# Attention and gated FFN in one kernel: VectorE forms the experts' input, GpSimd takes short row operations

## What is computed

```python
xn = (x - mean) / sqrt(var + 1e-5)                     # per row of 128
s  = causal attention of xn, 16 heads of 8, + xn, layer norm, gamma, beta
# key and query masks: rows of xn whose sum is exactly 0
xl = (xn - mean) * rsqrt(var + 1e-5) * ln_scale + ln_bias     # second norm
x_attn = xl @ attn_w.T + attn_b + xn                   # the experts' input, "xa"
h  = gelu(x_attn @ w1[e] + b1[e]); eo = h @ w2[e] + b2[e]      # 8 experts, 256 rows each
g  = silu(gelu(eo @ next_w.T + next_b))
out = x + s * g
```

## Time and profile before

| | before |
|---|---|
| median of 3 runs | 512.3 us (511.3 to 512.44) |
| the profiled execution, its own time | 512.2 us |
| its span | 510.4 us |
| PE busy | 430.7 us, 84% |
| DVE busy | 393.2 us, 77% |
| ACT busy | 301.9 us, 59% |
| POOL busy | 149.8 us, 29% |

### The profile page before, as it was taken

One profiled execution on the slowest core, in us unless ns is written; L12 is line 12 of the kernel. 1 busy time (PEld: TensorE's weight loads), 2 busy tenths in 40 slices (PEclk: granted clock), 3 DMA queues, 4 the chain that ended last, 5 costly groups with the idle time before them and its releaser, 6 DMA issues.

```text
span 510.4 us, 10343 instructions
## 1 busy us (share of the span) xinstructions
PE 430.7 (84%) x3731; PEld 267.3 (52%) x3731; DVE 393.2 (77%) x968; ACT 301.9 (59%) x644; POOL 149.8 (29%) x367
## 2 busy tenths in 40 slices
PE   0039903999999899999999999999999999999880
PEld 0016702777777655555555555555555555555430
DVE  6989988888994297769769769778778778778507
ACT  0127603788888517666666666666666666666760
POOL 8000000000000221121471471471472372373293
PEclk9999955899999999999999999999999999999995
DMA  8900300344443302312322322222222232130000
GB/s 224 312 5 0 84 1 7 81 130 129 128 118 98 88 4 50 95 49 57 82 56 70 84 62 70 76 69 70 75 71 69 68 79 71 55 90 23 4 21 21
DMA packets 27513, 37.60 MB, mean 74 GB/s; under 512 B 5686, under 2 KB 19910, under 8 KB 27462
## 3 DMA queue, kind: packets, MB, share of 16 engines
q1 hardware_dynamic: 27302, 36.92, 26.0%
q0 software_dynamic: 160, 0.03, 0.0%
HBM read 25.91 MB, written 10.49 MB: 71 GB/s over the span
## 4 chain that ended last, share of the span: by engine, by line
PE 50%; DVE 9%; POOL 2%; issue 2%; ACT 1%; DVEq 0%; ACTq 0%; POOLq 0%
PE banks L988 14%; PE banks L1019 13%; PE banks L1007 11%; DVE mx L833 5%; PE banks L990 5%; PE banks L1009 5%; PE banks L1029 1%; DVE stats L880 1%; PE banks L1073 1%; DVE aggr L884 1%; ACT pt L954 1%; ACT ots L938 0%; DVE seed L71 0%; DVE bits L70 0%; PE banks L997 0%
## 5 line engine op out<-in xcount | busy, mean ns | idle before, releaser
L833 DVE TENSOR_REDUCE mx<-banks 128x1 f32<-128x384 f32 (+3 forms) x384 | 210.1, 596 | 63.4 <-PE banks L990 58.0
L954 ACT ACTIVATE pt<-banks 128x512 f32<-128x512 f32 (+2 forms) x384 | 184.5, 527 | 101.9 <-PE banks L1009 90.5
L990 PE MATMUL banks<-causal,ident_b 128*128 128x128 bf16 x512 | 102.8, 220 | 0.0
L1009 PE MATMUL banks<-causalT,ident_b 128*128 128x128 bf16 x512 | 102.3, 219 | 0.0
L1019 PE MATMUL banks<-pt,vg 128*18 128x512 f32 (+3 forms) x1024 | 81.4, 436 | 1.3 <-ACT pt L954 1.3
L988 PE MATMUL banks<-w_room 73*128 73x512 bf16 (+3 forms) x256 | 69.0, 302 | 3.4 <-DVE mx L833 3.4
L988 PE MATMUL banks<-k_own,q_own 73*128 73x512 bf16 (+3 forms) x256 | 69.2, 302 | 3.0 <-DVE mx L833 2.5
L1007 PE MATMUL banks<-w_room 76*128 76x512 bf16 (+3 forms) x256 | 67.7, 300 | 1.5 <-ACT pt L954 1.5
L1007 PE MATMUL banks<-q_own,k_own 76*128 76x512 bf16 (+3 forms) x256 | 68.5, 300 | 0.2 <-ACT pt L954 0.2
L733 POOL TENSOR_SCALAR mneg<-mx 128x16 f32<-128x16 f32 x32 | 8.1, 255 | 168.1 <-DVEq L841 168.1
L990 PEld LDWEIGHTS banks<-causal,ident_b 128*128 128x128 bf16 x512 | 50.1, 98 | 0.9
(11 more groups left out here) (162 smaller groups left out, 635.1 us busy)
## 6 DMA issues: line engine op xcount, KB each, us to landing
k_scratch<-parts SPq DMA_DIRECT2D x40, 128.0 KB, 2.4
q_own<-q_scratch SPq DMA_DIRECT2D x48, 96.0 KB
k_own<-k_scratch SPq DMA_DIRECT2D x48, 96.0 KB
w_room<-q_scratch SPq DMA_DIRECT2D x48, 96.0 KB
w_room<-k_scratch SPq DMA_DIRECT2D x48, 96.0 KB
q_scratch<-parts SPq DMA_DIRECT2D x24, 128.0 KB, 2.4
w_room<-in_w_dram SPq DMA_DIRECT2D x1, 2048.0 KB, 9.6
out_dram<-mixed SPq DMA_DIRECT2D x7, 256.0 KB, 2.3
```

Source lines behind the costliest of these rows:

```text
L833: ins = dve.tensor_reduce(mx[:, u % 2, heads[0]:heads[-1] + 1, q], banks[:, S0 + c % RING, 0:w * len(heads)].rearrange("p (h k) -> p h k", ...
L954: act.activation(weights(k, heads[0], len(heads)), banks[:, ST0 + j % RING, 0:(T - P * k) * len(heads)], ACT.Exp, scale=SCALE).then_inc(ex ...
L990: ins = mm(o[:, w - P:w], ident_b[:, :], causal[:, :], start=False, stop=True)
L1009: ins = mm(o[:, 0:P], ident_b[:, :], causalT[:, :], start=False, stop=True)
```

## The change

TensorE's identity product of xnT is gone; VectorE computes xaT as bank XB + attn_b + xnT in one operation (`expert_input`), and ScalarE's `product_out` is gone. GpSimd gets the three Newton steps of the second roots (`second_roots`, 12 operations, once per group) and, per batch, `totals`: the four halvings of the row sum, and two operations for the shift of the second norm; VectorE keeps the seeds and the reduce and signals `seeds_ready` and `lanes_ready`. The mask operations are done once, at the end (`masks`). VectorE's order changes, and q, k and v of batch 0 stand ahead of its second norm.

```diff
+                def second_roots(tok, group):        # GpSimd
+                    at = slice(group[0], group[0] + group[1])
+                    pool.wait_ge(seeds_ready, tok.next(seeds_ready))
+                    for _ in range(3):
+                        link(tt(t2[:, at], y2[:, at], y2[:, at], ALU.mult))
+                        link(tt(t2[:, at], t2[:, at], v2[:, at], ALU.mult))
+                        link(pool.tensor_scalar(t2[:, at], t2[:, at], -0.5, 1.5, ALU.mult, ALU.add))
+                        link(tt(y2[:, at], y2[:, at], t2[:, at], ALU.mult))
+                def totals(tok, i):
+                    at = slice(TB * i, TB * i + TB)
+                    pool.wait_ge(lanes_ready, tok.next(lanes_ready))
+                    v = s16[:, at, :].rearrange("p n (a b l) -> p n a b l", a=2, b=2)
+                    link(tt(s8[:, at, :, :], v[:, :, :, 0, :], v[:, :, :, 1, :], ALU.add))
+                    link(tt(s4[:, at, :], s8[:, at, 0, :], s8[:, at, 1, :], ALU.add))
+                    v = s4[:, at, :].rearrange("p n (a b) -> p n a b", b=2)
+                    link(tt(s2[:, at, :], v[:, :, :, 0], v[:, :, :, 1], ALU.add))
+                    link(tt(rem[:, at], s2[:, at, 0], s2[:, at, 1], ALU.add))
+                    link(pool.tensor_scalar(shift[:, at], rem[:, at], -1.0 / C, None, ALU.mult))
+                    link(tt(shift[:, at], shift[:, at], y2[:, at], ALU.mult))
+                    pool.sem_inc(sums_ready, 1)
+                for i in range(B):
+                    if i == 0:
+                        second_roots(tok, GROUPS[0])
+                    if i == 2:
+                        second_roots(tok, GROUPS[1])
+                    totals(tok, i)
...
+                def expert_input(i):                 # VectorE
+                    dve.wait_ge(xnT_ready, i + 1)
+                    dve.wait_ge(xa_done, i + 1)
+                    dve.scalar_tensor_tensor(out=xaT[:, :], in0=banks[:, XB, :], scalar=attn_b, in1=xnT[:, i % 2, :],
+                                             op0=ALU.add, op1=ALU.add).then_inc(xaT_ready, 1)
...
                         link(ins)
+                        if term == 1 and i > 2:
+                            expert_input(i - 1)
...
                 def sums(i):
-                    row_sum(link, dve, rem[:, tiles], ...
-                    link(dve.scalar_tensor_tensor(out=norm2[:, i, 1], ...
-                    link(dve.tensor_copy(norm2[:, i, 0], y2[:, tiles]))
-                    dve.sem_inc(sums_ready, 1)
-                    link(dve.tensor_scalar(zero_all[:, tiles], rem[:, tiles], 0.0, None, ALU.is_equal))
+                    dve.tensor_reduce(s16[:, tiles, :], xn_all[:, tiles, :].rearrange("p n (k l) -> p n l k", l=16),
+                                      AX.X, ALU.add).then_inc(lanes_ready, 1)
...
                 quotients(0)
-                second_roots(GROUPS[0])
+                second_seeds(GROUPS[0])
                 sums(0)
                 quotients(1)
                 sums(1)
                 dve.wait_ge(x_in[1], 16)
                 rests(tok, 0)
                 means(GROUPS[1])
+                expert_input(0)
+                variances(GROUPS[1])
                 lows(tok, 0)
-                variances(GROUPS[1])
+                expert_input(1)
                 roots(GROUPS[1])
+                second_seeds(GROUPS[1])
+                rests(tok, 1)
                 for i in range(2, B):
                     quotients(i)
-                    rests(tok, i - 1)
-                    if i == 2:
-                        second_roots(GROUPS[1])
                     sums(i)
-                    if i == B - 1:
...
+                    if i > 2:
+                        rests(tok, i - 1)
                     lows(tok, i - 1)
+                expert_input(B - 1)
+                masks()
                 rests(tok, B - 1)
                 lows(tok, B - 1)
...
                 tok = Tokens(act)                    # ScalarE
                 norm_out(tok, 0)
+                split(tok, 0)
                 second_norm(tok, 0)
                 second_out(tok)
-                product_out(tok)
...
                 def attn_product(tok, n):            # TensorE
                     pe.wait_ge(xlT_ready, tok.next(xlT_ready))
-                    mm(banks[:, XB, :], wattn_sb[:, :], xlT[:, :], start=True, stop=False)
-                    pe.wait_ge(xnT_ready, tok.next(xnT_ready))
-                    mm(banks[:, XB, :], ident[:, :], xnT[:, n % 2, :], start=False, stop=True).then_inc(xa_done, 1)
+                    mm(banks[:, XB, :], wattn_sb[:, :], xlT[:, :], start=True, stop=True).then_inc(xa_done, 1)
+                    if n > 0:
+                        pe.wait_ge(xnT_ready, tok.next(xnT_ready))
...
                 normed(tok, 0)
+                pe.wait_ge(xnT_ready, tok.next(xnT_ready))
+                projections(tok, 0)
                 second_normed(tok, 0)
                 attn_product(tok, 0)
```

More of the change, by code:

```diff
@@ L193, in build_program @@
         xl_st = s1("xl_st", [P, 2, TB, C])
-        norm2 = s1("norm2", [P, B, 2, TB])
+        shift = s1("shift", [P, NT])
         xnT = s1("xnT", [P, 2, T])
@@ L229, in build_program @@
             "mask_ready", "maskT_done", "maskT_ready", "mask_out"))
-        mean, var, a, y, t, s, sh, sl, r, nr, rem, v2, y2 = (small[:, k, :] for k in range(13))
+        mean, var, a, y, t, s, sh, sl, r, nr, rem, v2, y2, t2 = (small[:, k, :] for k in range(14))
         with nc.Block() as block:
@@ L377, in quotients @@
                     link(tt(qlo[:, :, :], quo[:, :, :], qhi[:, :, :], ALU.subtract))
-                    for in0, by, in1, op, dst in (
+                    for term, (in0, by, in1, op, dst) in enumerate((
                             (qhi, sh, cu, ALU.subtract, wu), (qlo, sh, wu, ALU.add, wu),
                             (qhi, sl, wu, ALU.add, wu), (qlo, sl, wu, ALU.add, wu),
-                            (wu, nr, quo, ALU.add, xn_all[:, tiles, :])):
+                            (wu, nr, quo, ALU.add, xn_all[:, tiles, :]))):
                         for k in range(TB):
@@ L488, in gelu_out, with split @@
                                    ACT.Gelu).then_inc(vb_free, 1)
-                    if i < B - 1:
-                        product_out(tok)
[L492 to L498, removed]
+                def split(tok, i):
                     for o, bias, done in ((0, bq, q_done), (1, bk, k_done)):
@@ L510, in _ @@
                                    ACT.Relu).then_inc(vb_free, 1)
+                tok = Tokens(act)
+                norm_out(tok, 0)
+                split(tok, 0)
+                second_norm(tok, 0)
+                second_out(tok)
+                for i in range(B):
+                    n, last = i % STEPS, i == B - 1
+                    if i > 0:
+                        split(tok, i)
                     if last:
@@ L554, in second_normed, with projections @@
                     ins.then_inc(trl_done, 1)
+                def projections(tok, i):
+                    xT = xnT[:, i % 2, :]
+                    mm(banks[:, QB, :], wq_sb[:, :], xT, start=True, stop=True).then_inc(q_done, 1)
+                    mm(banks[:, KB, :], wk_sb[:, :], xT, start=True, stop=True).then_inc(k_done, 1)
+                    pe.wait_ge(vb_free, tok.next(vb_free))
+                    if i == 0:
+                        pe.wait_ge(bias_ready, 1)
+                    bias_first(0)
+                    for k in range(TB):
+                        ins = mm(banks[:, VB, P * k:P * k + P], xT[:, P * k:P * k + P], wv_sb[:, :],
+                                 start=False, stop=(k == TB - 1))
+                    ins.then_inc(v_done, 1)
                 def attn_product(tok, n):
                     pe.wait_ge(xlT_ready, tok.next(xlT_ready))
[L558 to L565 removed]
+                    mm(banks[:, XB, :], wattn_sb[:, :], xlT[:, :], start=True, stop=True).then_inc(xa_done, 1)
+                    if n > 0:
+                        pe.wait_ge(xnT_ready, tok.next(xnT_ready))
                 def bias_first(row):
@@ L579, in next_product @@
                     ins.then_inc(next_done, 1)
+                tok = Tokens(pe)
+                normed(tok, 0)
+                pe.wait_ge(xnT_ready, tok.next(xnT_ready))
+                projections(tok, 0)
+                second_normed(tok, 0)
+                attn_product(tok, 0)
                 for i in range(B):
                     n = i % STEPS
[L583 to L593, removed]
+                    if i > 0:
+                        projections(tok, i)
                     if i == B - 1:
```

25 lines of the change are left out of this document (13 added, 12 removed).

## The result

The changed kernel took **506.64 us** (median of 4 runs, 506.03 to 507.34) against 512.37 for the kernel before; ratio 0.9893, 95% interval 0.9875 to 0.9912. That is 5.7 us less, outside the range of the forecast (510.9, 507.3 to 514.7). The profiled execution took 507.34, with a span of 505.5; it is the slowest of the four. Some executions show a lower granted clock and take some 3% longer (of the kernels here, two executions of one, 522 us); ratios and medians leave them out.

The account below looks back on a forecast made before the run. Bound: VectorE's front, then a VectorE-ScalarE loop of 14.0 per batch, not TensorE (12.85). Batch 7's w1 products start at 164.5 for 165.93, 1.4 us earlier, stage two unchanged: 510.9, range 507.3 to 514.7.

Parts of the forecast that it names:

- W(7): Start of batch 7's w1 products on TensorE, forecast at 164.5 against 165.93 before, 1.4 us earlier.
- W(2): Start of batch 2's w1 products on TensorE, forecast at 94.4 against 97.35 before.
- (5): Front, engine sharing: VectorE pays 0.05 per GpSimd operation, 1.5 us; GpSimd waits for VectorE's operation in flight, totals over at 84.5.
- (3): Steady batches: a closed loop over VectorE and ScalarE, quotients to quotients, sets a pace of 14.0, 0.3 above the former pace.
- the last way: From VectorE's xaT(6), over at 148.5, through batch 7's attention product at 161.6 to W(7) at 164.5.
- Rival A: VectorE pays 0.20, GpSimd's whole short operation, each time: slower, 516.0; chance 0.12.
- (4): VectorE's front from 26.53 to the reduce of batch 2, summed to 78.8 before sharing costs.
- W(0): Start of batch 0's w1 products on TensorE, forecast to move from 43.77 to 47.
- The wait for xaT(1): Front: VectorE reaches its sum for batch 1 at 59.7 to 60.7, the attention product is there at 60; costs up to 1.
- The premise of an unchanged stage two: Everything behind stage one is left as it is; stage two must take the same 332.5 us.
- Rival B: No sharing costs between VectorE and GpSimd: W(7) at 160.3, 5.6 earlier, time 506.7; chance 0.10.
- D: Rival: GpSimd's totals later by d in every batch; 1 us gives 5.6 more than the forecast, 516.5; chance 0.13.

## Why the prediction was wrong

The way that the time takes was right; terms of the sum were mis-sized. W(7) was forecast at 164.5 and came at 161.78, 2.7 earlier: 1.4 at W(2), from (5), and 1.3 behind it, from (3) and the last way. Stage two adds 0.8 and the placing of the profiled execution 0.7.

- **(3), the loop: right in mechanism, mis-sized.** VectorE and ScalarE hold each other at 13.75, forecast 13.98, and the identity product turned into waits. Two terms were too long: the sum, 0.66 from start to start for 0.75, and the reduce, 0.94 for 1.06, because neither is followed by a wait for itself any more, so the next one starts before it has ended. Four loops make 1.0 of W(7); the last way, from xaT(6) to W(7), took 15.5 for 16.0.
- **(5), what VectorE pays: the step that failed first.** I took 0.05 for each of 29 operations, 1.5 us, from a row beside 256-element copies; measured 0.2 in all. The reduce of batch 2 ended at 79.0, forecast 80.3, and the error of W(2), 93.02 for 94.4, follows from it. Rival A, built on the whole 0.20, is refuted for short operations. The trace before held a row that I passed over, a short VectorE operation of 0.48 at 11.37, beside a 256-column GpSimd product that ended with it: this row and those of the last section show that VectorE pays more where GpSimd's operation is longer.
- **(5), what GpSimd pays: right beside long operations.** Totals of batch 2 over 3.9 us after the reduce (forecast 4.2). Beside the terms it pays almost nothing, where I had let each one wait for the operation in flight; it did not matter.
- **(4), the front: right, in part by luck.** W(0) at 46.74 and the cold first products (6.53 for 3.62) are as written. The wait for xaT(1), 0.70, was named ("up to 1") but not in the sum of 78.8; that the sum held is luck, since the other terms came 0.7 shorter together. The product that VectorE waited for also adds up to 59.3 by the terms given there, not the 60 written; it came at 59.9.
- **The premise of an unchanged stage two: wrong by 0.8.** W(7) came 4.15 earlier, forecast 1.4. With 0.8 that stage two took less (331.7 for 332.5) and 0.7 by which the profiled execution lies above its median, this is the whole distance from 510.9 to 506.6. Of the 0.8, 0.3 is there from its second batch on, which I can't explain, and 0.5 arises at TensorE's last four transposes, for which the granted clock was 0.50 in the kernel before and 1.00 in the changed one (rows in the last section).
- Rival B's number, 506.7, which the range left out, was hit by luck: GpSimd did wait, W(2) was 93.02 and not B's 90.5, and the front, the pace, stage two and the median only happened to add up to the same. D's danger was real and is what the first rest ahead of the reduce showed; the changed kernel stood 0.4 us away from it, since VectorE came to its sum at 104.25 and TensorE's product had ended at 103.87.

The Trainium skill (SBUF — State Buffer, "Who interferes with whom") lets the first to issue hold the shared pair for the whole instruction. For GpSimd's waiting the traces agree, beside both kinds of VectorE operation with two SBUF inputs (0.63 to 0.74). For VectorE's they agree where GpSimd's operation is long, as the next section shows, and a short one costs VectorE too little to be seen as a whole 0.20.

## To carry to other kernels

Where two engines wait for each other inside a batch, add the starts round the loop before counting what an engine is relieved of: 0.86 us off TensorE, the busiest engine, was worth nothing, and 24 operations of 0.2 us off the front of VectorE were worth all of the gain. Short work that goes to GpSimd belongs beside reduces (0.20 to 0.22 each beside the reduce of the means, at 39.3 us) or short VectorE operations; beside 512-column operations with two inputs it takes three times as long. And a wait of TensorE near 2 us can cost most of its length again through the clock (1.6 behind 2.06), though not each time.

## What the runs showed that I had not expected

VectorE does wait for all of a long GpSimd operation. In the kernel before, VectorE's 32-column product took 0.99 in the last batch, 0.19 in the one at 233.12, while this ran on GpSimd:

```profile
498.00 0.99 DVE L851 TENSOR_TENSOR rec<-rec,live_all 128x32 f32<-128x32 f32 x1
```

```profile
497.69 1.26 POOL L782 TENSOR_TENSOR mix<-gate,half 128x512 f32<-128x512 f32 x1
```

It ends with GpSimd's. In the changed kernel a four-column `tensor_scalar` of the last batch met the same and took 1.13 for 0.17:

```profile
496.38 1.13 DVE L915 TENSOR_SCALAR seed<-aggr 128x4 f32<-128x4 f32 x1
```

Which operation is hit differs, but not the price: from the last reciprocal to VectorE's last row it is 10.52 us before and 10.60 after. So this is not where stage two's 331.5 to 332.5 comes from. TensorE's last transposes are, in the kernel before and in the changed one:

```profile
496.45 1.12 PE L1029 MATMUL banks<-ident,ots 128*128 128x128 f32 x4 [0.72 <-ACT ots L938]
```

```profile
491.99 0.66 PE L1083 MATMUL banks<-ident,ots 128*128 128x128 f32 x4 [0.72 <-ACT ots L992]
```

Three kernels have them at half clock, 1.08 to 1.12: the one before, the one with the identity product back and the one with rests and lows as another kind. Their stage two took 332.2 to 332.5; in nine others, at 0.65 or 0.66, it took 331.5 to 331.8. What sets the clock there no run tested. In stage one too: TensorE's granted clock fell after idle times of 2.06 us in one kernel and stayed after 2.14 us in another.
